# Carrying the last group's normalised heads into the rows of the others by transfers, in an attention and feed-forward kernel

## The chip, the cores and the metric
One core of a Trainium2 chip runs the whole program. The metric is the device time of one execution in microseconds (us). The engines are PE (TensorE, matrix products), DVE (VectorE), ACT (ScalarE), POOL (GpSimd) and SP (SyncE, which here only issues transfers). Each has a queue of its own that it works in order; they meet at semaphores.

## The reference
Input x is 2 x 2048 x 256 in float32. What is computed, cut down:

```
Q, K, V = x Wq^T, x Wk^T, x Wv^T          # 16 heads of 16 columns
O = causal softmax(Q K^T / 4) V, per head  # blocks of 128 keys in the reference
x = layernorm(x + O Wo^T)
lhs_scale = max|x| over a row / 127 ; rhs_scale = max|F| over a column / 127
acc = round(x / lhs_scale) @ round(F / rhs_scale)   # int8 values, clipped to 127
x = layernorm(x + acc * lhs_scale * rhs_scale)
```

## The kernel before
**Groups and steps.** The 2 x 16 heads are worked off as 8 groups of 4 heads (HG). A group covers one batch's 2048 tokens in 4 chunks of 512 queries (CH); chunk c meets key blocks kb = 0 to 4c + 3. This gives NS = 40 steps a group, 320 in all (ALL); FIRST = 0, 4, 12, 24 are the steps at which the chunks start in a group. In the last 4 steps of a chunk the width falls from 512 to 384, 256 and 128 (the diagonal). Step k issues on PE four score products, one for each head (L681, `product`), with three PSUM banks in turn; ACT takes the exponential of each (L1003) into PR. The products with the values (L734, `values_half`) follow two steps later (LAG) in two halves, behind scores 1 and 3. They add up in one bank, ps_acc, where head j has the rows from 32j: 16 rows of outputs and 16 of the sum of exponentials.

**Row maxima.** In groups 0 to 6 the queue of PE also holds, between the scores, the products for the row maxima of the next group (L681 into ps_max, `item`), which DVE reduces (L1072). The last group has none of them.

**The accumulator.** When a chunk's last values product is done, ACT copies ps_acc to accS[:, c % 2] (`copy_acc`, L993). This copy stands in ACT's queue behind the exponential of head 3 of the next chunk's step kb = 1. The first values product of the next chunk (step kb = 0, issued in step kb = 2) waits for it. In groups 0 to 6 SP then stores the four heads and the sums to DRAM (L456, L458).

**Ends of chunks.** When all 16 heads of a chunk of tokens are there, the chunk m (0 to 7, four of each batch) goes through projection with Wo, residual, layernorm, quantising, product with the int8 weights, residual, layernorm and store. This is done by halves of 256 tokens, e = 2m + s. Every operation of a half has a due step, written out in tables: HALF_START[e] plus an entry of DUE[e]. Each engine calls its part for the step that it is in (`end_parts` on DVE, ACT, POOL and SP; `between_scores` on PE in the last group). Within one step an engine does later stages of earlier halves first. Chunks 0 to 2 are worked within groups 4 to 6, chunk 3 at the start of the last group (halves 6 and 7 start at its steps 0 and 2).

**The joined chunks 4 to 7 (JOINED).** Their last four heads come from the last group itself. The 12 other heads are loaded from DRAM to o_in (128 rows in half h = 0, 64 rows in h = 1) and normalised by POOL with inverses spread in DRAM (`outputs`, L1383). The last four stay in accS: PE sums them to tokens by four small products with the tile `spread` (`token_sums`, L887), DVE inverts (`invert_last`, L1218, L1220), PE spreads the inverses over accS's rows by products with ident (`spread_inverses`, L899), DVE multiplies (`normalise_last`, L1226). The projection (`project`, `tiled`, L824) of one tile of 128 tokens is then three sets of four 32-column products: o_in half 0, o_in half 1 with 64 rows, and accS with wo_last, a copy of Wo's last 64 rows at the rows of accS (made by four transfers at the start). A half has two tiles. Of the joined chunks, 4, 5 and 6 have their copies at steps 5, 13 and 25 of the last group (COPIED), and their halves start at 7 and 9, 15 and 17, 27 and 29; token sums come at step 6, 14 and 26, spreads at the start of each half. Chunk 7 comes after the last score: its projection of o_in is done beforehand (L870) and finished with wo_last behind the others (`finish_projection`, L909).

**Order within a step of the last group.** Behind score j: `project` of tile j // 2 and half h = j % 2; with j = 0 the token sums and spreads (`joins`) and the turning of integers (`late_turn`, L845); with j = 2 the int8 product (`late_product`, L824 with ffn_q); with j = 1 and 3 the values.

Of the kernel before, what the change touches and what calls it, by code (L numbers as in the profile page):

```python
# [61 lines left out]
def build(nc, x, wq, wk, wv, wo, ffn, out):  # L62
# [45 lines left out]
    LAST_GROUP = (GROUPS - 1) * NS  # L108
    SOON_START = [NS * (GROUPS // B - 1 + m) + 26 for m in range(SOON)]
    JOINED = range(CHUNKS, ENDS)  # L110
    COPIED = [LAST_GROUP + FIRST[c] + 1 for c in range(1, CHUNKS)] + [ALL - 1]
    HALF_START = [at for at in SOON_START for s in range(2)] + [LAST_GROUP, LAST_GROUP + 2] + \
        [at for k in COPIED[:-1] for at in (k + 2, k + 4)] + [ALL + 1, ALL + 2]
    soon_chunk = lambda at: dict(sums_in=at - 17, sums_back=at - 14, load=at - 7, outputs=at - 2)
    CHUNK_DUE = [soon_chunk(at) for at in SOON_START] + [
        {part: LAST_GROUP + k for part, k in zip(("sums_in", "sums_back", "load", "outputs"), at)}
# [2 lines left out]
    def steps_of(**at):  # L119
# [10 lines left out]
                     product=28, residual2=29, rstd2=34, store=37)]  # L130
    LATE_DUE = dict(steps_of(mean=2, norm=4, mean2=11, norm2=13, gap=0), project0=0, project1=1, rstd1=3, to_int=6, turn=7,
                    take=7, product=8, scale=9, residual2=10, rstd2=12, store=14)
    JOIN_DUE = dict(LATE_DUE, spread=0, normalise=0, project0=1, project1=1)
    LAST_DUE = dict(LATE_DUE, spread=0, normalise=0, project0=-2, project1=-2, finish=1)
    DUE = [SOON_DUE[e % 2] if e < SOON_HALVES else LATE_DUE if e // 2 not in JOINED else JOIN_DUE if e < 2 * ENDS - 2
           else LAST_DUE for e in range(2 * ENDS)]
    DONE_AT = max(HALF_START[e] + max(DUE[e].values()) for e in range(2 * ENDS))

# [7 lines left out]

    def joins_due(k):

        return [m for m in JOINED if HALF_START[2 * m] - 1 == k]

    soon_due = lambda k, part: [e for e in due(k, part) if e < SOON_HALVES]
    late_due = lambda k, part: [e for e in due(k, part) if e >= SOON_HALVES]
# [109 lines left out]
    with ExitStack() as ctx:  # L262
# [89 lines left out]
        e_wo = sem("wo_last_in")  # L352
        e_wo_set = sem("last_constants")
        e_token = sem("sums_by_token")
        e_spread = sem("inverses_spread")
        e_last = sem("last_outputs_normalised")
        groups_under = lambda m: -(-(SLOT[m] - 1) * 3 * W // (TILES * GR))
# [35 lines left out]
        QSTEPS = 3 + TPH + 1  # L393
        late = lambda e: e - SOON_HALVES
        LAST_STEPS = 4
        joined = lambda m: m - JOINED[0]
        banks_of = lambda m: ps_score if m == ENDS - 1 else ps_max
        token_bank = lambda m: banks_of(m)[:, 0, 0:TPC * HG]
        spread_bank = lambda m, s: banks_of(m)[:, s, 0:HALF]
# [33 lines left out]
        with nc.Block() as block:  # L433
            @block.sync
            def _(sp):
# [43 lines left out]
                def end_parts(k):  # L479
                    for m in chunks_due(k, "sums_in"):  # L480
                        sums_in(m)
                    for m in chunks_due(k, "sums_back"):
                        sums_back(m)
                    for m in chunks_due(k, "load"):
                        load(m)
                    for e in due(k, "store"):
                        store_result(e)

# [39 lines left out]
                def load(m):  # L528
                    b, t0 = place(m)
                    if SLOT[m] >= 2:  # L530
                        sp.wait_ge(s_vg, CHUNKS * groups_under(m))
                    at_least(sp, e_out[SLOT[m]], 2 * 16 * (nth(m) - 1))
                    sp.wait_ge(e_back[SLOT[m]], 16 * nth(m))
                    for h in range(HALVES):
                        r, n = b * HEADS + h * (HEADS // HALVES), half_rows(m, h)
                        sp.dma_start(inv_in(m)[0:n, h, :], row_inv[m % CHUNKS, r:r + n // DH, :].unsqueeze(1)
                                     .broadcast_to([n // DH, DH, CH])).then_inc(e_in[SLOT[m]], 16)
                        sp.dma_start(o_in(m)[0:n, h, :], heads_out[r * DH:r * DH + n, t0:t0 + CH])\
                            .then_inc(e_in[SLOT[m]], 16)
                    sp.dma_start(work(m), x[b, t0:t0 + CH, :].rearrange("(t p) d -> p t d", p=P))\  # L540
                        .then_inc(e_x[SLOT[m]], 16)

                def sums_of(rows, m):

# [31 lines left out]
            def _(pe):  # L576
# [198 lines left out]
                def between_scores(k, j):  # L775


                    at = NS * (GROUPS - 1) + k
                    project(at, j // 2, j % 2)
                    if j == 0:  # L780
                        joins(at)
                        late_turn(at)
                    if j == 2:
                        late_product(at)
                    if j % 2:
                        values_half(*divmod(at - LAG, NS), j // 2)

                def soon_parts(k):

# [64 lines left out]
                def project(k, t, h):  # L854


                    for e in late_due(k, f"project{t}"):
                        m, s = divmod(e, 2)
                        if t == 0 and h == 0:
                            pe.wait_ge(e_on, HALVES * (m + 1))  # L860
                            pe.wait_ge(s_reduced, NI * GROUPS)
                            pe.wait_ge(e_res, e - 1)
                            if e == 2 * JOINED[0]:
                                pe.wait_ge(e_wo, 16 * HG)
                            if m in JOINED and m < ENDS - 1:
                                pe.wait_ge(e_last, LAST_STEPS * joined(m) + 3 + s)
                        at, n = s * HALF + t * P, half_rows(m, h)
                        rows = ps_max[:, s, t * D:t * D + D]
                        if m == ENDS - 1:
                            pe.matmul(rows, o_in(m)[0:n, h, at:at + P], wT[0:n, 3, h, :], start=t == 0 and h == 0, stop=False)  # L870
                            continue
                        last = h == HALVES - 1
                        y = tiled(rows, o_in(m)[0:n, h, at:at + P], wT[0:n, 3, h, :], h == 0, last and m not in JOINED)
                        if last and m in JOINED:
                            y = tiled(rows, accS[:, m % 2, at:at + P], wo_last[:, :], False, True)
                        if last:
                            y.then_inc(e_y, 1)

                def token_sums(m):
# [24 lines left out]
                def finish_projection(e):  # L904
                    m, s = divmod(e, 2)
                    pe.wait_ge(e_last, LAST_STEPS * joined(m) + 3 + s)
                    for t in range(TPH):
                        at = s * HALF + t * P
                        pe.matmul(ps_max[:, s, t * D:t * D + D], accS[:, m % 2, at:at + P],  # L909
                                  wo_last[:, :], start=False, stop=t == TPH - 1).then_inc(e_y, 1)  # L910
# [22 lines left out]
            def _(act):  # L933
# [53 lines left out]
                def copy_acc(g, c):  # L987
                    act.wait_ge(s_pv, NS * g + LAST[c] + 1)
                    if g < GROUPS - 1 or c < 2:
                        at_least(act, s_ost[c % 2], OST * (CHUNKS // 2 * g + c // 2))  # L990
                    else:
                        act.wait_ge(e_y, TPH * late(2 * (JOINED[c - 2] + 1)))
                    act.copy(accS[:, c % 2, :], ps_acc[:, :]).then_inc(s_accS, 1)  # L993

                def group(g):
                    for k, (c, kb) in enumerate(STEPS):
                        w = CH - skip(c, kb)
                        for j in range(HG):
                            use = score_use(g, k, j)
                            act.wait_ge(s_st, use + 1)  # L1000
                            if j == 0:
                                at_least(act, s_pv, NS * g + k - 3)
                            act.activation(PR[:, k % 4, j, 0:w], ps_score[:, bank_of(use), 0:w], ACT.Exp,  # L1003
                                           scale=SCALE).then_inc(s_exp, 1)
                            if kb == 1 and j == HG - 1 and (g or c):
                                copy_acc(g if c else g - 1, (c - 1) % CHUNKS)
                        soon_parts(NS * g + k)
                        end_parts(NS * g + k)
# [422 lines left out]
```

## Time and profile before
| | us |
|---|---|
| median of 3 runs (lowest, highest) | 1008.3 (1007.88, 1009.81) |
| the profiled execution | 1007.38 |
| its span in the trace | 1005.7 |
| busy: PE, DVE, ACT, POOL | 944.5, 799.5, 719.9, 272.0 |
| front part, up to the first steady group | about 120 |
| steady groups | 98 to 105 each |
| from step 4 of the last group to its last score | 863.74 to 976.11 |

The profile shows one execution. The profiled execution's own time is 1.7 us above its span; what lies between is start and end around the recorded work. A "quad" is four products of 32 columns each that run side by side in PE; a quad in float32 is recorded as 8 matmuls (two records for each), one in bf16 as 4. "x8" in a row of PE counts such records. The time of a row ends with its last record, which overlaps the next row; what a quad occupies is the distance between starts.

### The profile page before, as it was taken

What the parts mean: (1) busy time and instruction counts of PE and PEld (TensorE: products, weight loads), DVE (VectorE), ACT (ScalarE), POOL (GpSimd) and SP (SyncE); (2) the same over time, 40 slices, a digit from 0 to 9 for tenths busy, and PEclk for the clock granted to TensorE, in tenths of its full rate; (3) what the DMA queues carried; (4) which work ended last, traced back from release to release, by engine and by line L of the source; (5) the groups of instructions that cost most, each with busy time, mean ns of one, the idle gap of its engine ahead of it and who ended that gap; (6) DMA issues with size and microseconds to landing.
All of it is one profiled execution on the core that took longest, in us unless ns stands there. A gap on an engine that the chain in (4) does not pass through costs nothing.

```text
span 1005.7 us, 41095 instructions
## 1 busy us (share of the span) xinstructions
PE 944.5 (94%) x18208; PEld 590.9 (59%) x18208; DVE 799.5 (80%) x1081; ACT 719.9 (72%) x1494; POOL 272.0 (27%) x443
## 2 busy tenths in 40 slices
PE   8989999999999999999999999999999999879993
PEld 5645556656765676566656675666666654444441
DVE  5488888887888788878889898999899899365426
ACT  3423458788788878887878877887787887757670
POOL 4433452102210221021213230333124212353322
PEclk9999999999999999999999999999999999989995
DMA  5565440002210220022302230124013114502101
GB/s 177 161 200 159 157 125 15 5 9 53 69 32 9 60 68 24 9 58 80 83 6 60 64 116 8 40 76 114 19 34 78 50 33 112 114 14 75 34 2 42
DMA packets 70865, 66.47 MB, mean 66 GB/s; under 512 B 14704, under 2 KB 65200, under 8 KB 70688
## 3 DMA queue, kind: packets, MB, share of 16 engines
q1 hardware_dynamic: 70688, 63.84, 22.8%
q8 instruction: 143, 2.34, 1.0%
q14 instruction: 34, 0.28, 0.1%
HBM read 42.43 MB, written 20.91 MB: 63 GB/s over the span
## 4 chain that ended last, share of the span: by engine, by line
PE 77%; DVE 10%; ACT 6%; SPq 3%; issue 2%; POOL 1%; DMA 1%; POOLq 0%; ACTq 0%; DVEq 0%
PE ps_acc L734 20%; PE ps_score L681 19%; PE ps_max L681 18%; DVE block_max L1072 6%; PE ps_score L604 5%; ACT PR L1003 4%; PE ps_score L611 3%; PE ps_max L824 2%; PE ps_max L679 2%; SPq L439 2%; PE ps_max L699 2%; PE ps_score L824 1%; ACT accS L993 1%; PE ps_acc L585 1%; DVE end_slots L1183 1%
## 5 line engine op out<-in xcount | busy, mean ns | idle before, releaser
L1072 DVE TENSOR_REDUCE block_max<-ps_max 128x2 f32<-128x1024 f32 (+3 forms) x640 | 654.3, 1059 | 113.3 <-PE ps_max L681 56.7
L1003 ACT ACTIVATE PR<-ps_score 128x512 f32<-128x512 f32 (+3 forms) x1280 | 627.2, 539 | 160.4 <-PE ps_score L681 141.7
L681 PE MATMUL ps_score<-QS,KS 99*32 99x512 bf16 (+3 forms) x5120 | 452.3, 350 | 3.3 <-ACT PR L1003 2.2
L734 PE MATMUL ps_acc<-PR,VG 128*32 128x256 f32 (+1 forms) x5104 | 367.7, 350 | 10.5 <-ACT accS L993 9.1
L681 PE MATMUL ps_max<-KS,QS 96*32 96x512 bf16 (+3 forms) x4544 | 335.1, 348 | 5.5 <-DVE block_max L1072 2.9
L681 PEld LDWEIGHTS ps_score<-QS,KS 99*32 99x32 bf16 x5120 | 169.4, 96 | 96.5 <-ACT PR L1003 22.5
L734 PEld LDWEIGHTS ps_acc<-PR,VG 128*32 128x32 f32 x5104 | 170.2, 110 | 83.7 <-ACT PR L1003 16.2
L681 PEld LDWEIGHTS ps_max<-KS,QS 96*32 96x32 bf16 x4544 | 138.5, 96 | 88.4 <-DVE block_max L1072 37.7
L1318 POOL TENSOR_SCALAR_AFFINE_SELECT PR<-PR 128x512 f32<-128x512 f32 x128 | 82.8, 647 | 284.3 <-ACT PR L1003 284.1
L699 PE MATMUL ps_max<-mask_q,ident_b 128*32 128x96 bf16 (+3 forms) x1808 | 99.1, 200 | 0.0
L699 PEld LDWEIGHTS ps_max<-mask_q,ident_b 128*32 128x32 bf16 x1808 | 60.7, 97 | 10.0
L1326 POOL CAST max_parts<-neg_max 16x128 bf16<-16x128 f32 (+1 forms) x30 | 8.9, 297 | 195.1 <-ACT neg_max L985 193.1
L604 PE MATMUL ps_score<-PR,wT 128*128 128x512 f32 x128 | 60.3, 597 | 0.8 <-ACT neg_max L963 0.8
L945 ACT CAST end_slots<-ps_score 128x512 bf16<-128x512 f32 x32 | 18.7, 585 | 56.7 <-PE ps_score L604 56.7
L1305 POOL TENSOR_TENSOR end_slots<-PR,end_slots 128x512 bf16<-128x512 f32 x32 | 37.0, 1155 | 78.3 <-ACT end_slots L950 78.3
L679 PE MATMUL ps_max<-KS,QS 96*128 96x512 bf16 (+3 forms) x144 | 35.9, 345 | 7.1 <-DVE block_max L1072 7.0
L604 PEld LDWEIGHTS ps_score<-PR,wT 128*128 128x128 f32 x128 | 23.3, 190 | 20.6 <-issue 18.0
L1355 POOL TENSOR_SCALAR var_eps<-moments 128x2 f32<-128x2 f32 x32 | 7.4, 231 | 86.3 <-DVE moments L1178 86.3
L611 PE MATMUL ps_score<-wT,PR 128*128 128x256 f32 x128 | 30.0, 381 | 0.0
L1172 DVE BATCH_NORM_STATS2 stats<-end_slots 128x6 f32<-128x256 f32 x48 | 19.0, 417 | 12.0 <-POOL end_slots L1374 11.8
L1121 DVE TENSOR_TENSOR PR<-ps_score,end_slots 128x512 f32<-128x512 f32 x32 | 21.7, 683 | 8.0 <-ACT end_slots L945 6.9
L679 PEld LDWEIGHTS ps_max<-KS,QS 96*128 96x128 bf16 x144 | 13.3, 97 | 24.3 <-DVE block_max L1072 13.1
(125 smaller groups left out, 558.5 us busy)
## 6 DMA issues: line engine op xcount, KB each, us to landing
QS<-qparts SPq DMA_DIRECT2D x192, 64.0 KB, 2.4
KS<-kparts SPq DMA_DIRECT2D x192, 64.0 KB, 2.3
qparts<-end_slots SPq DMA_DIRECT2D x16, 384.0 KB, 3.8
kparts<-end_slots SPq DMA_DIRECT2D x16, 384.0 KB, 3.1
PR<-in_L_attn_x SPq DMA_DIRECT2D x8, 512.0 KB, 4.3
heads_out<-accS SPq DMA_DIRECT2D x112, 32.0 KB
end_slots<-in_L_attn_x SPq DMA_DIRECT2D x6, 512.0 KB, 7.5
out_y<-end_slots SPq DMA_DIRECT2D x12, 256.0 KB, 2.1
```

Source lines behind the costliest of these rows:

```text
L604: m = pe.matmul(bank, wT[:, w, mh, nh * P:nh * P + P], xT[:, n % 2, mh, :], start=mh == 0, stop=mh == HALVES - 1)
L611: m = pe.matmul(bank[:, t * D:t * D + D], xT[:, n % 2, mh, tile * P:tile * P + P], wT[:, 2, mh, :], start=mh == 0, stop=mh == HALVES - 1)
L679: return pe.matmul(bank[:, 0:w], stack, moving, start=True, stop=stop)
L681: m = pe.matmul(bank[t * QW:t * QW + QW, 0:w], stack[:, t * QW:t * QW + QW], moving, start=True, stop=stop)
L699: m = pe.matmul(bank[r:r + QW, w - P + r:w], ident_b[:, r:r + QW], mask_q[:, r:P], start=False, stop=True)
L734: m = pe.matmul(ps_acc[EYE * j:EYE * j + EYE, a:b], VG[:, kb, j, :], PR[:, k % 4, j, a - s:b - s], start=kb == 0 and a == 0, stop=k == LAS ...
L824: y = pe.matmul(out[r:r + QW], stack[:, r:r + QW], moving, start=start, stop=stop)
L1003: act.activation(PR[:, k % 4, j, 0:w], ps_score[:, bank_of(use), 0:w], ACT.Exp, scale=SCALE).then_inc(s_exp, 1)
L1072: dve.tensor_reduce(block_max[:, h * PAIR:h * PAIR + PAIR, i, b], ps_max[:, slot_at:slot_at + PAIR, 0:w], AX.X, ALU.max).then_inc(s_reduce ...
L1121: dve.tensor_tensor(rest[:, q % RESTS, :], ps_score[:, u % 3, :], parts[:, n % 2, u, 0, :], ALU.subtract)\
L1305: pool.tensor_tensor(parts[:, n % 2, u, 2, :], rest[:, q % RESTS, :], parts[:, n % 2, u, 1, :], ALU.subtract).then_inc(part3, 1)
L1318: pool.affine_select(out=block, in_=block, compare_op=ALU.is_ge, fill=0.0, base=0, pattern=[[0, HG], [1, P]], channel_multiplier=-1).then_ ...
```

## The change
Four edits:
1. For chunks 4 to 6, when both halves of accS have been multiplied, SP copies the four heads' rows by four transfers (`join_heads`) into the rows 64 to 127 of o_in half 1, which were unused. The projection of these chunks is then two sets of products with 128 rows; the products with wo_last are left to chunk 7 alone. PE waits for the transfers (e_join) before a half's first projection, and ACT's copy to a buffer that was joined waits for them too.
2. These halves start three steps later (10 and 12, 18 and 20, 30 and 32), their two tiles are projected in two steps, and both halves are spread in one step (7, 15, 27) and multiplied in the next (8, 16, 28), where the transfers are due too. Everything else of these halves moves three steps later with them: the last of chunk 6 comes to steps beyond the last score.
3. Token sums and spreads stand behind the values at the end of a step (j = 3), the turning of integers behind score 3.
4. In all groups, the copy of the accumulator stands behind the exponential of head 2 of its step, not of head 3.

```diff
-        [at for k in COPIED[:-1] for at in (k + 2, k + 4)] + [ALL + 1, ALL + 2]
+        [at for k in COPIED[:-1] for at in (k + 5, k + 7)] + [ALL + 1, ALL + 2]
...
-    JOIN_DUE = dict(LATE_DUE, spread=0, normalise=0, project0=1, project1=1)
+    JOIN_DUE = [dict(LATE_DUE, spread=-3, normalise=-2), dict(LATE_DUE, spread=-5, normalise=-4, join=-4)]
...
-        return [m for m in JOINED if HALF_START[2 * m] - 1 == k]
+        return [m for m in JOINED if COPIED[joined(m)] + 1 == k]
...
+                    for e in due(k, "join"):
+                        join_heads(e // 2)
                     for e in due(k, "store"):
                         store_result(e)
...
+                def join_heads(m):
+
+                    sp.wait_ge(e_last, LAST_STEPS * (joined(m) + 1))
+                    for j in range(HG):
+                        r = P - GR + j * DH
+                        sp.dma_start(o_in(m)[r:r + DH, HALVES - 1, :], accS[EYE * j:EYE * j + DH, m % 2, :])\
+                            .then_inc(e_join, 16)
...
-                    if j == 0:
-                        joins(at)
-                        late_turn(at)
                     if j == 2:
                         late_product(at)
+                    if j == 3:
+                        late_turn(at)
                     if j % 2:
                         values_half(*divmod(at - LAG, NS), j // 2)
+                    if j == 3:
+                        joins(at)
...
-                            if e == 2 * JOINED[0]:
-                                pe.wait_ge(e_wo, 16 * HG)
                             if m in JOINED and m < ENDS - 1:
-                                pe.wait_ge(e_last, LAST_STEPS * joined(m) + 3 + s)
-                        at, n = s * HALF + t * P, half_rows(m, h)
+                                pe.wait_ge(e_join, 16 * HG * (joined(m) + 1))
+                        at, n = s * HALF + t * P, half_rows(m, h) if m == ENDS - 1 else P
...
-                        last = h == HALVES - 1
-                        y = tiled(rows, o_in(m)[0:n, h, at:at + P], wT[0:n, 3, h, :], h == 0, last and m not in JOINED)
-                        if last and m in JOINED:
-                            y = tiled(rows, accS[:, m % 2, at:at + P], wo_last[:, :], False, True)
-                        if last:
+                        y = tiled(rows, o_in(m)[0:n, h, at:at + P], wT[0:n, 3, h, :], h == 0, h == HALVES - 1)
+                        if h == HALVES - 1:
                             y.then_inc(e_y, 1)
...
-                        act.wait_ge(e_y, TPH * late(2 * (JOINED[c - 2] + 1)))
+                        act.wait_ge(e_join, 16 * HG * (c - 1))
...
-                            if kb == 1 and j == HG - 1 and (g or c):
+                            if kb == 1 and j == HG - 2 and (g or c):
                                 copy_acc(g if c else g - 1, (c - 1) % CHUNKS)
```

## Rows read from the trace of the kernel before

**Rows 1.** The page: busy time, share of the span and instructions.
```profile
PE 944.5 (94%) x18208; PEld 590.9 (59%) x18208; DVE 799.5 (80%) x1081; ACT 719.9 (72%) x1494; POOL 272.0 (27%) x443
```

**Rows 2.** Busy time by stretch: start:end, length, engines, PE clock, DMA share, GB/s.
```profile
550.00:655.00 105.00, 102.65 (x2320) 67.66 (x2312) 94.03 (x126) 85.32 (x184) 30.24 (x54) 1.00 0.22 60
863.74:976.11 112.37, 99.16 (x1729) 50.38 (x1717) 57.58 (x169) 79.01 (x163) 39.03 (x57) 0.94 0.21 52
```

**Rows 3.** Waits of PE and weight loads, 120 to 868: total, times, longest.
```profile
PE ps_acc L734 <- ACT accS L993: 9.1, 21, 0.6
...
PEld ps_max L681 <- DVE block_max L1072: 37.7, 113, 1.1
```

**Rows 4.** Timeline, a copy within a group: start, length, what [idle before].
```profile
250.35 0.22 PE L734 MATMUL ps_acc<-PR,VG 128*32 128x64 f32 x1
...
251.01 0.58 ACT L993 COPY accS<-ps_acc 128x512 f32<-128x512 f32 x1
...
251.73 0.64 PE L734 MATMUL ps_acc<-PR,VG 128*32 128x256 f32 x8 [0.49 <-ACT accS L993]
```

**Rows 5.** Timeline, the last values product before a copy at a group's start.
```profile
242.47 0.29 PE L734 MATMUL ps_acc<-PR,VG 128*32 128x64 f32 x8
```

**Rows 6.** Waits of PE, 862 to 985, the last group.
```profile
PE ps_max L899 <- DVE last_sums L1220: 4.0, 1, 4.0
PE ps_max L887 <- ACT accS L993: 3.5, 3, 1.2
PE ps_max L845 <- ACT end_slots L1051: 2.3, 3, 0.9
PE ps_max L845 <- ACT V L1051: 1.1, 2, 0.8
...
PE ps_max L824 <- DVE accS L1226: 0.7, 1, 0.7
```

**Rows 7.** Timeline of PE and weight loads, one tile's projection.
```profile
878.84 0.61 PE L824 MATMUL ps_max<-wT,V 128*32 128x256 f32 x8
879.27 0.62 PE L824 MATMUL ps_max<-ffn_q,end_slots 128*32 128x256 bf16 x16
...
880.03 0.15 PEld L824 LDWEIGHTS ps_max<-wT,V 64*32 64x32 f32 x8 [0.32 <-issue]
...
880.60 0.64 PE L824 MATMUL ps_max<-wo_last,accS 128*32 128x256 f32 x8
```

**Rows 8.** Timeline of ACT, three plain steps.
```profile
955.06 5.99 ACT L1003 ACTIVATE PR<-ps_score 128x512 f32<-128x512 f32 x12 [1.19 <-PE ps_score L681]
```

**Rows 9.** Busy time by stretch, as rows 2, one of three where the clock is low.
```profile
903.23:906.70 3.47, 3.47 (x52) 2.23 (x56) 1.07 (x3) 1.19 (x2) 0.00 (x0) 0.50 0.11 35
```

**Rows 10.** Normalising, issue (ns min/median/max), landing (KB each, median us).
```profile
875.82 0.41 DVE L1226 TENSOR_TENSOR accS<-accS,ps_max 128x256 f32<-128x256 f32 x1
...
L456 SPq DMA_DIRECT2D heads_out<-accS x112: 303/421/1669, 152.9 to 861.9; - x112
...
wo_last<-wT SPq DMA_DIRECT2D x4, 16.0 KB, 2.4
...
end_slots<-in_L_attn_x SPq DMA_DIRECT2D x2, 512.0 KB, 8.3
```

**Rows 11.** The chain of waits from the last values to half 14.
```profile
977.29 2.51 PE ps_max L870 x8
...
985.33 0.70 DVE end_slots L1272
```

**Rows 12.** The same chain, later.
```profile
996.49 1.07 PE ps_max L824 x14
997.58 0.89 DVE end_slots L1248 x2
998.54 1.27 POOL end_slots L1374
999.84 0.76 DVE stats L1172 x2
```

More of the change, by code:

```diff
@@ L110, in build @@
     JOINED = range(CHUNKS, ENDS)
+    joined = lambda m: m - JOINED[0]
     COPIED = [LAST_GROUP + FIRST[c] + 1 for c in range(1, CHUNKS)] + [ALL - 1]
     HALF_START = [at for at in SOON_START for s in range(2)] + [LAST_GROUP, LAST_GROUP + 2] + \
-        [at for k in COPIED[:-1] for at in (k + 2, k + 4)] + [ALL + 1, ALL + 2]
+        [at for k in COPIED[:-1] for at in (k + 5, k + 7)] + [ALL + 1, ALL + 2]
     soon_chunk = lambda at: dict(sums_in=at - 17, sums_back=at - 14, load=at - 7, outputs=at - 2)
@@ L132, in build @@
                     take=7, product=8, scale=9, residual2=10, rstd2=12, store=14)
-    JOIN_DUE = dict(LATE_DUE, spread=0, normalise=0, project0=1, project1=1)
     LAST_DUE = dict(LATE_DUE, spread=0, normalise=0, project0=-2, project1=-2, finish=1)
-    DUE = [SOON_DUE[e % 2] if e < SOON_HALVES else LATE_DUE if e // 2 not in JOINED else JOIN_DUE if e < 2 * ENDS - 2
+    JOIN_DUE = [dict(LATE_DUE, spread=-3, normalise=-2), dict(LATE_DUE, spread=-5, normalise=-4, join=-4)]
+    DUE = [SOON_DUE[e % 2] if e < SOON_HALVES else LATE_DUE if e // 2 not in JOINED else JOIN_DUE[e % 2] if e < 2 * ENDS - 2
            else LAST_DUE for e in range(2 * ENDS)]
@@ L354, in build @@
         e_token = sem("sums_by_token")
+        e_join = sem("last_heads_joined")
         e_spread = sem("inverses_spread")
@@ L395, in build @@
         LAST_STEPS = 4
-        joined = lambda m: m - JOINED[0]
         banks_of = lambda m: ps_score if m == ENDS - 1 else ps_max
@@ L906, in finish_projection @@
                     pe.wait_ge(e_last, LAST_STEPS * joined(m) + 3 + s)
+                    if s == 0:
+                        pe.wait_ge(e_wo, 16 * HG)
                     for t in range(TPH):
```

## The prediction
> **What bounds the kernel now.** I began with the page: TensorE (PE) is busy for 94% of the span, ACT for 72%, and nothing else comes near [rows 1]. So the question is where PE has time that it loses. The table by stage splits it: in a steady stretch PE is busy for 102.65 of 105 us, in the stretch of the last group from step 4 to the last score, 863.74 to 976.11, for 99.16 of 112.37 us, at a mean clock of 0.94 [rows 2]. A steady group is one long PE queue. What PE itself waits for there is nearly one thing, the copy of the accumulator: 9.1 us in 21 waits [rows 3]. After the last score comes a chain of some 29 us across DVE, POOL, ACT and PE, in which every step counts [rows 11, 12]. The three stretches are costed apart. All terms are for the profiled execution: 1007.4 us with a span of 1005.7; the median of the runs is 1008.3, 0.9 more, and I add the change to that median.
>
> **The copy one head sooner (groups 0 to 6, and the joins between them).** The copy stands in ACT's order behind the exponential of head 3. At 251 us the last product of values of the old chunk ends near 250.6, yet the copy begins at 251.01, when the exponential of head 3 is through, and PE takes up the next product of values at 251.73, having waited 0.49 [rows 4]. One exponential takes 0.49 of ACT's queue (12 in 5.99, less the overlap of the last [rows 8]), so with the copy ahead of it PE finds the buffer free when it comes: the 0.49 goes. The exponential of head 3 ends when the copy ended before, and PE asks for its bank behind the next values product, past 252.1, so nothing replaces the wait. Not so where the chunk copied is the fourth of a group: the values product started at 242.47 and ran for 0.29, so the copy can't start before 242.8 wherever it stands, and it did start then [rows 5]; there PE's wait stays, and the exponential behind it comes 0.4 later, which PE's next scores just bear. Three of the 21 waits are of that kind (at the longest, 0.6, 1.7 us). 18 waits with 7.4 us can go. Some of it PE will hand on, since weight loads for the row maxima stand 37.7 us behind DVE [rows 3] and in the later groups DVE is busy for 94.03 of 105 us [rows 2]. Ends: 2 (DVE absorbs most) and 8; I take 5.5, near the upper one, since DVE has slack even there. **-5.5.**
>
> **The last group: waits of PE that go.** PE waits 3.5 us in three token sums for the copy, 4.0 in one spread for DVE's inverse, 0.7 for DVE's normalising, 2.3 and 1.1 in turns for ACT's integers [rows 6]. Token sums move from the start to the end of the step after the copy, about 1.7 us of PE work later, and the copy is a head sooner: all 3.5 go. The spread of 4.0 waited because DVE was inside the norm-to-round block of the half before, which started its step earlier; now the projections start three steps later, so at that join DVE has only second norms left: 4.0 goes. The 0.7 goes with its wait. Turns stand behind score 3 now, whose bank is free only after the integers were made; but 1.9 of their 3.4 us lie between 960 and 968, where ACT sets the pace (below), so I take 1.0 of them. **-9.2.**
>
> **The products with wo_last.** One tile's projection was three groups in PE: heads 0 to 7 (878.84 to 879.27, 0.43), the 64 rows of the other half (880.03 to 880.60, 0.57, with about 0.1 lost ahead of it), and accS with wo_last (0.46); the weights of the 64-row group are not loaded ahead, its load row shows a gap of 0.32 [rows 7]. Together 1.57 us. With 128 full rows it is twice 0.43, 0.87: 0.70 less for a tile, and there are 12 such tiles (96 matmuls of wo_last, 8 for each): 8.4 us of PE work. What it is worth hangs on the step. A plain step is 8 quads of scores and values, 1.74 us of PE, while ACT's four exponentials take 1.96 to 2.0 (12 in 5.99 and PE paced by them) [rows 8]: there ACT is the bound. Before, both tiles of a half fell into one step: 1.74 + 3.13 = 4.87 of PE, and the step behind it was ACT's, 1.96: 6.83. Now the tiles fall into two steps of 1.74 + 0.87 = 2.61: 5.22. Six halves: 6 x 1.6 = **-9.7.** The normalise work of POOL and DVE is unchanged in amount. Bounds: 5 (if the weight gaps stay and ACT hides part) and 10.
>
> **The clock.** After the idle time at the token sums and the spread, PE ran at the half level (granted 0.50, that is 1.2 GHz) from 903.23 to 906.70 [rows 9]; there are three such stretches of 3.0 to 3.5 us in the last group, about 9.9 us in all, and half of it, 4.9 us, is lost. The idle time that goes is what came before these falls. Two thirds of it, **-3.2**: a new wait (next part) can make it fall once. The Trainium skill, "TensorE: Matmul & The Clock Gate", What's actually happening, has the same two levels and an idle stretch as the cause; by that rule a join that stops PE for long would bring the loss back, which is part of rival B.
>
> **The joins.** Each of three chunks adds four transfers of 32 KB on SP's queue and a wait of PE at the first projection. The chain: spreads at the end of a step; two normalises of 0.41; four issues at 0.42 each (1.7, as for the same rows into heads_out); a landing, for which the nearest row is the load of wo_last, also from SBUF to SBUF, 2.4 us; the lower end is a transfer that PE never waits for, the upper a landing of 8.3 (tokens, 512 KB) [rows 10]. I take 2.4, since the queues are quiet there (a DMA share of 0.21 [rows 2]). Sum 0.8 + 1.7 + 2.4 + 0.3 for handing over = 5.2 us. PE gets to the first projection after two steps and a score. A step takes the larger of ACT's 1.96 (0.5 more where it makes integers or takes a turn) and PE's 1.74 (0.43 more for an int8 product): 2.5 and 2.0 for steps 8 and 9 of the last group (chunk 4), 2.5 and 2.4 for 16 and 17, 2.2 and 2.0 for 28 and 29: 4.2 to 4.9, plus 0.2. For chunk 4 DVE is late besides: it norms to 875.8 as before [rows 10]. So the three waits are about 1.6, 0.4 and 1.0: **+3.0**, bounds 0 and 3 x 6 = 18. Behind the waiting projection PE holds scores, so ACT runs dry with it. Behind the join on SP stand the stores of finished halves and chunk 7's load, with steps to spare; ahead of chunk 5's stands the store of half 6 (step 14), whose norm is due at 13. [...]
> The copies of chunks 6 and 7 now wait for the joins of 4 and 5, due eight steps and more earlier: nothing.
>
> **Sum of the last group:** -9.2 - 9.7 - 3.2 + 3.0 = -19.1. 112.4 becomes 93.3, still above ACT's 79.0 busy [rows 2].
>
> **The tail.** Chunk 6 starts three steps later, so the product of its second half and DVE's work on both halves move behind the last score. (1) The product stands in PE's queue between the projection of 977.29, which ends at 979.80, and the token sums [rows 11]: 0.62 at full clock [rows 7], 1.07 at half [rows 12]; I take 0.6, since its overlap with the neighbours is worth some of the slower clock. (2) DVE's queue ahead of the residual of half 14 (985.33 [rows 11]) held one norm, one pair of stats and two normalises, and it still waited for L909. Now PE's token sums end at about 981.4, inverse and first spread at 982.7, then: normalise 0.4, stats and aggregate of half 12 0.76 + 0.25, two scalings 0.85 [rows 12], which ends at 984.9; POOL's residual of half 13 follows, behind its rstd, 0.2 + 1.27 to 986.35 [rows 12]; then stats and aggregate 0.95: the residual starts at 987.3 instead of 985.33, +2.0, with (1) in it. (3) Norm 2 of half 13 now stands ahead of norm 1 of half 14: +0.65. Together **+2.7**; ends 0.6 (only the product) and 5 (all 4.3 of moved DVE work and the product).
>
> **Total:** -5.5 - 19.1 + 2.7 = -21.9; 1008.3 - 21.9 = 986.4.
>
> **Rivals.** (A) The copy gains nothing in the steady groups: DVE, busy for up to 90% there, takes over the waits, or the held exponential costs what the copy gives. For it: 37.7 us of weight loads behind DVE [rows 3]; against: 11 us of 105 in which DVE is idle [rows 2]. The rest as forecast: -16.4, 992. (B) The wait at the joins takes the place of those removed: landings of 4 to 5 us, each wait 3 to 4, the clock falls as before and the 3.2 is not had: -21.9 + 8 + 3.2 = -10.7, 998. For it: the chain has no reserve at any of the three; against: wo_last's 2.4 [rows 10]. (C) The better end: the clock stays up all through, joins cost nothing, 7.4 is had: -21.9 - 1.9 - 1.7 - 3.0 = -28.5, 980. (D) Slower: the join on SP. It is one queue in order; if a join is held behind the store ahead of it or lands as the tokens do, at 8.3 us, PE stops 6.9 us at each and runs at half clock for 3.5 us behind each (1.75 lost): 3 x 8.65 = 26 instead of 3, no clock gain: -21.9 + 23 + 3.2 = +4.3, 1012.6. It decides from a landing of about 7 us. Against it: no transfer of this size behind so little traffic takes as long. That the change doesn't do what it says is hard to see: 96 matmuls leave PE whatever happens.
>
> **How the numbers follow.** Forecast (984 to 989.5) 0.38, A 0.17, B 0.21, C 0.17, D 0.03, and 0.04 for mishaps beyond these, shared by the three outcomes. The range from 979 to 999 holds C, A and most of B. A measurement of this kernel tells 0.2% (2 us) from no change: faster 0.94, same 0.02, slower 0.04.
>
> **What would show it.** No waits of L734 on accS but those at a group's start; no matmul with wo_last but in the tail; h=1 projections with 128 rows and no gap of the weight load; PE waits at L824 for the join of about 1 us; the clock at 1.00 from 890 on; 93 us from step 4 of the last group to its last score; the tail from the last value product to the end 2 to 3 us longer. Wrong if DVE waits of PE grow in the steady groups, if the join waits are above 3 us, or if the clock falls at other places.

## The result and the profile after

The changed kernel takes 991.8 us (median of 4 runs, 990.22 to 994.13) where the kernel before took 1008.45: a ratio of 0.9835, 95% interval 0.9812 to 0.9858, or 16.6 us less. The forecast was 21.9 us less: 986.4, in a range of 979 to 999. The profiled execution took 992.43 us with a span of 990.7, 15.0 less than the span before.

The page (shares as in [rows 1]), then the busy time by stretch (columns as in [rows 2]); the second stretch runs, as there, from step 4 of the last group to the last values:

```profile
PE 935.6 (94%) x18112; PEld 589.1 (59%) x18112; DVE 799.9 (81%) x1081; ACT 716.3 (72%) x1494; POOL 271.9 (27%) x443
```
```profile
550.00:655.00 105.00, 103.76 (x2361) 68.67 (x2352) 95.26 (x126) 86.08 (x185) 31.38 (x56) 1.00 0.22 62
861.42:958.25 96.83, 88.66 (x1616) 49.97 (x1604) 55.24 (x163) 76.93 (x162) 38.24 (x56) 0.96 0.25 64
```

PE has 96 records fewer, those of wo_last. In the steady stretch PE is busy for 103.76 of 105 us (102.65 before), in the last group for 88.66 of 96.83 (99.16 of 112.37): the stretch shrank by 15.5 us and PE's work by 10.5.

The best ruler is ACT's copy of the accumulator, which both kernels make 32 times: the same copy marks the same place of the work in both. These are the copies of chunks 4 to 7 in the last group of the changed kernel, from ACT's timeline (start, length, idle before; the first row is the last copy of group 6):

```profile
856.89 0.58 ACT L1002 COPY accS<-ps_acc 128x512 f32<-128x512 f32 x1 [0.47 <-PE ps_acc L745]
866.43 0.63 ACT L1002 COPY accS<-ps_acc 128x512 f32<-128x512 f32 x1
887.87 0.58 ACT L1002 COPY accS<-ps_acc 128x512 f32<-128x512 f32 x1 [0.26 <-PE ps_acc L745]
921.99 0.58 ACT L1002 COPY accS<-ps_acc 128x512 f32<-128x512 f32 x1 [0.61 <-PE ps_acc L745]
959.50 0.58 ACT L1002 COPY accS<-ps_acc 128x512 f32<-128x512 f32 x1 [0.56 <-PE ps_acc L745]
```

| us | before | after | difference | forecast |
|---|---|---|---|---|
| first copy to the last of group 6 | 707.38 (152.26 to 859.64) | 704.97 (151.92 to 856.89) | -2.4 | -5.5 |
| first to last copy of the last group | 108.46 (868.90 to 977.36) | 93.07 | -15.4 | -19.1 |
| last copy to the end of the span | 28.3 | 31.2 | +2.9 | +2.7 |

**The steady groups.** PE's waits from 120 to 865 us, as in [rows 3]:

```profile
PE ps_max L692 <- DVE block_max L1081: 5.0, 9, 2.7
PE ps_score L692 <- ACT PR L1012: 3.0, 8, 0.6
PE ps_acc L745 <- ACT accS L1002: 1.8, 4, 0.5
```

Of 21 waits for the copy 4 are left, and their sum fell from 9.1 to 1.8 us. The copy of [rows 4] looks like this now, and there is no wait at the values product behind it (timeline: the last product of the old chunk, the copy, the first of the new one):

```profile
249.51 0.22 PE L745 MATMUL ps_acc<-PR,VG 128*32 128x64 f32 x1
...
249.81 0.58 ACT L1002 COPY accS<-ps_acc 128x512 f32<-128x512 f32 x1
...
250.54 0.64 PE L745 MATMUL ps_acc<-PR,VG 128*32 128x256 f32 x8
```

The lead over the kernel before is how much sooner the same copy starts. Within a group it grows by 0.3 to 0.5 us from copy to copy, at a group's start it shrinks by 0.25. At the copy of 445.66 it is 2.62, at 466.14 (469.87 before) 3.73. At the next, 499.82 (500.48), it is 0.66. Between them lies one long wait, the 2.7 of the first row above:

```profile
464.05 0.43 SPq L563 DMA_DIRECT2D sums<-row_sums  x1
...
467.33 0.20 DVE L1166 TENSOR_SCALAR sums<-sums 128x64 f32<-128x64 f32 x1 [2.29 <-DMA sums<-row_sums]
...
468.98 0.61 PE L692 MATMUL ps_max<-KS,QS 96*32 96x512 bf16 x8 [2.71 <-DVE block_max L1081]
```

DVE stood 2.29 us at the sums of chunk 0 for a transfer that SP issued at 464.05 and that was there at 467.3; PE then stood 2.71 us for DVE's maxima. Behind that wait the granted clock of PE fell (first row below, columns as in [rows 2]: 0.62 on average over the stretch; the other two rows are of the last group):

```profile
469.00:473.50 4.50, 4.50 (x55) 1.93 (x58) 2.03 (x3) 2.28 (x4) 0.00 (x0) 0.62 0.34 82
896.42:900.80 4.38, 4.38 (x52) 2.36 (x44) 4.08 (x13) 3.84 (x8) 1.01 (x2) 0.61 0.12 26
921.40:924.40 3.00, 3.00 (x46) 1.39 (x48) 2.83 (x11) 2.41 (x6) 1.72 (x3) 0.57 0.26 87
```

**The last group.** PE's waits from 862 us on, as in [rows 6] (the lines that matter for chunks 4 to 7; 9.0 us of the first is in the tail):

```profile
PE ps_max L857 <- ACT end_slots L1060: 9.5, 2, 9.0
PE ps_score L692 <- ACT PR L1012: 2.1, 3, 1.4
PE ps_max L906 <- DVE V L1281: 1.9, 1, 1.9
PE ps_acc L745 <- POOL PR L1327: 1.8, 2, 1.3
PE ps_max L836 <- ACT end_slots L1050: 1.4, 2, 0.7
PE ps_max L836 <- POOL V L1392: 1.0, 1, 1.0
...
PE ps_max L836 <- DMA end_slots<-accS: 0.4, 1, 0.4
```

The token sums' 3.5, the normalising's 0.7 and the turns' waits in the group are gone. In place of the spread's 4.0 stand 1.9 for a residual (L1281), and new is a score that waits 1.4 for ACT, at 920.46. Where that comes from, DVE and ACT say (timeline):

```profile
919.29 0.63 ACT L1060 ACTIVATE V<-V 128x512 bf16<-128x512 f32 x1 [1.26 <-DVE V L1221]
...
920.46 0.55 PE L692 MATMUL ps_score<-QS,KS 99*32 99x512 bf16 x4 [1.39 <-ACT PR L1012]
```

ACT stands 1.26 us for DVE's rounding of half 10, with its exponentials queued behind; PE has filled its three banks and stands too. Part of DVE's lateness is a meeting with POOL. The small product for lscale takes DVE 0.17 us at 893.32 and 899.19; here it takes 1.08 and ends when POOL's residual of another half ends (timeline):

```profile
916.53 1.27 POOL L1383 TENSOR_TENSOR V<-V 128x512 f32<-128x512 f32 x1
...
916.75 1.08 DVE L1206 TENSOR_SCALAR lscale<-amax 128x2 f32<-128x2 f32 x1
```
That is 0.9 of the 1.26 us. The joins cost about 1.4: 1.0 at chunk 4 (the table gives it to POOL's L1392, which ended at about the same time; that instruction is chunk 5's, and most later executions put the same wait down to the transfer) and 0.4 at chunk 6.

A tile's projection is now two sets with 128 rows (881.82 and 882.31, each with another product behind it). There is no gap, and a set occupies 0.43 to 0.44 us:

```profile
881.82 0.64 PE L836 MATMUL ps_max<-wT,V 128*32 128x256 f32 x8
882.25 0.27 PE L692 MATMUL ps_score<-QS,KS 99*32 99x128 bf16 x4
882.31 0.64 PE L836 MATMUL ps_max<-wT,V 128*32 128x256 f32 x8
882.75 0.53 PE L745 MATMUL ps_acc<-PR,VG 128*32 128x192 f32 x8
```

**The tail.** The chain of waits from the last copy on, as [rows 11]:

```profile
961.95 0.55 PE ps_max L836 x16
962.50 1.00 PE ps_score L894 x8
...
967.24 1.67 DVE end_slots L1192 x2
968.91 0.67 DVE stats L1181 x2
...
969.85 0.59 DVE end_slots L1281
```

The int8 product stands ahead of the token sums (0.55), then DVE's norm and statistics of halves 12 and 13 ahead of the residual of half 14. That residual starts 10.3 us behind the last copy; before it was 8.0 (977.36 to 985.33). The norm of 967.24 is another meeting with POOL, whose residual runs from 967.18 to 968.44: 1.67 us, where two such operations take 0.73 elsewhere in the tail.

### The profile page after: what moved, and what is told of

Its sections match the earlier page's. It is cut to its first block, busy times and chain, and to the rows that moved or that the text cites. A ratio compares the mean times of both kernels' runs of the same rounds, so it can differ in the third digit from the quotient of the medians.

```text
span 990.7 us, 40916 instructions
## 1 busy us (share of the span) xinstructions
PE 935.6 (94%) x18112; PEld 589.1 (59%) x18112; DVE 799.9 (81%) x1081; ACT 716.3 (72%) x1494; POOL 271.9 (27%) x443
## 4 chain that ended last, share of the span: by engine, by line
PE 77%; DVE 10%; SPq 6%; ACT 3%; issue 2%; POOL 1%; DMA 1%; POOLq 0%; DVEq 0%; ACTq 0%
PE ps_acc L745 20%; PE ps_score L692 20%; PE ps_max L692 18%; DVE block_max L1081 6%; PE ps_score L615 5%; SPq L440 4%; PE ps_score L622 3%; PE ps_max L690 2%; ACT PR L1012 2%; PE ps_max L836 2%; PE ps_max L710 1%; PE ps_score L836 1%; SPq L457 1%; PE ps_acc L596 1%; DVE end_slots L1192 1%
## 5 line engine op out<-in xcount | busy, mean ns | idle before, releaser
L1192 DVE TENSOR_SCALAR end_slots<-end_slots,moments,rstd 128x256 f32<-128x256 f32 x48 | 20.9, 459 | 9.4 <-POOL rstd L1367 9.4
```

The costliest lines, as they stand in the source:

```text
L1192: dve.tensor_scalar(dst[:, at, :], src[:, at, :], moments[:, z, which, at, 0:1], rstd[:, z, which, at:at + 1], ALU.subtract, ALU.mult).the ...
```

## The experiments

Eleven kernels in three rounds. Those of a round shared their runs of the kernel before, whose medians were 1008.07 us (experiments 1 to 4), 1006.88 (5 to 8) and 1008.06 (9 to 11). A difference of about 1 us between medians of different rounds is therefore not safe; each ratio is to the kernel before in its own round.

**1. The copy alone.** On the kernel before:
```diff
-                            if kb == 1 and j == HG - 1 and (g or c):
+                            if kb == 1 and j == HG - 2 and (g or c):
```


> The kernel before with one edit of the four alone: the accumulator is copied behind the exponential of head 2. Theory (the copy's gain builds up at 0.3 to 0.5 us a copy until about 470 us, 3.7 us by then in the changed kernel, and is then given back where DVE waits for the sums' transfer): by the end of group 6 about 2.5 us earlier than before, and in the last group the three token sums still wait, but 0.5 us less each; in all 3 to 5 us, 1004. Rival (DVE takes over the waits everywhere, and the steps of the last group gain nothing from the copy): 1 us at most, 1007.5. As the prediction had it (5.5 in the steady groups): 1002.

Measured: 1001.21 us, ratio 0.9928 (0.9901 to 0.9955). First copy to the last of group 6: 702.19, 5.2 us less; last group 107.5, 1.0 less; tail the same. The prediction's 5.5 fits. The idea of the expectation, that the gain is given back at the sums as a consequence of the copy, fell here: this kernel has the copy and waited only 0.37 us for the sums.

**2. All but the copy.** The changed kernel with the reverse of that edit.

> The changed kernel with the copy put back behind the exponential of head 3. Theory: the steady groups lose their 2.3 us and the 3.1 us given back at 470 to 500 don't arise, because DVE then comes to the sums after they have landed; the first values product of chunks 1 to 3 in the last group waits 0.5 longer each. In all 2.5 to 4 us slower than the changed kernel, 995. Rival (the copy is worth nothing, the last group all): 992, the same as the changed kernel.

Measured: 997.61, ratio 0.9889 (0.9858 to 0.9919): 5.8 slower than the changed kernel. And DVE waited 2.5 us for the sums, without the sooner copy: the steady groups took 4.3 us more than in the kernel before. So the wait hangs on when the transfer lands. In the thirteen profiled executions of this document it was there 1.9 to 2.1 us after its issue in ten, and 3.3 to 3.5 in three (the changed kernel, experiment 2, and the kernel of experiment 9). The program around it is the same in the changed kernel and in experiment 4, where it came early:

```profile
463.95 0.42 SPq L563 DMA_DIRECT2D sums<-row_sums  x1
465.90 0.20 DVE L1171 TENSOR_SCALAR sums<-sums 128x64 f32<-128x64 f32 x1 [0.43 <-DMA sums<-row_sums]
```
The two rows are experiment 4's. What makes the landing late in some executions stays open.

**3. The inverses later,** on the changed kernel:
```diff
-    soon_chunk = lambda at: dict(sums_in=at - 17, sums_back=at - 14, load=at - 7, outputs=at - 2)
+    soon_chunk = lambda at: dict(sums_in=at - 17, sums_back=at - 12, load=at - 7, outputs=at - 2)
```


> The changed kernel with the inverses of the first batch's sums two steps later on DVE (sums_back at - 12 instead of at - 14), so that DVE comes to them after the transfer has landed. Theory (a wait of DVE for the sums of 2.3 us, taken over by PE as 2.7 us and paid again in 3 us at the half clock, gave back 3.1 us of the copy's gain): no wait of DVE for the sums, no half clock at 470 to 474, the end 3 us sooner, 989, and the start of step 4 of the last group 5.4 us earlier than in the kernel before instead of 2.3. Rival (DVE is the bound of groups 4 to 6 and takes over whatever comes free): the wait goes, and the end stays at 991 to 992.

Measured: 989.72, ratio 0.9812 (0.9785 to 0.9839). DVE inverts at 468.35 without a wait; the first copy is at 152.02, the last of group 6 at 852.78: 700.76, 6.6 less than before. This execution alone doesn't show that the two steps of reserve help, since its transfer landed after 1.9 us. The kernel of experiment 9 shows it: it has the later inverses too, and its transfer landed 3.3 us after the issue, at 468.5, still ahead of DVE:

```profile
465.19 0.43 SPq L569 DMA_DIRECT2D sums<-row_sums  x1
...
468.99 0.18 DVE L1172 TENSOR_SCALAR sums<-sums 128x64 f32<-128x64 f32 x1
```
It lost nothing there: 701.08 us from the first copy to the last of group 6. The median of experiment 3 is 2.1 better, less than the 3 expected. That would fit a wait that not every execution has, but the intervals of the two ratios overlap, so the size of the gain is not settled.

**4. wo_last kept.** The changed kernel without `join_heads`, with the projection's third set of products as before:
```diff
-                                pe.wait_ge(e_join, 16 * HG * (joined(m) + 1))
+                                pe.wait_ge(e_last, LAST_STEPS * joined(m) + 3 + s)
...
+                        if last and m in JOINED:
+                            y = tiled(rows, accS[:, m % 2, at:at + P], wo_last[:, :], False, True)
```


> The changed kernel with the products of wo_last kept in the projections of chunks 4 to 6 and no transfers to o_in; steps, order and copy as changed. Theory of the prediction (the 12 times 0.70 us of PE work are worth their full amount, since all twelve lie in steps that PE bounds, less the waits for the transfers of 1.4 us that go): 6 to 7 us slower than the changed kernel, 998.5. Rival (the steps and waits made the gain, ACT covers the work): within 2 us of the changed kernel, 993.

Measured: 992.77, ratio 0.9846 (0.9819 to 0.9873), 1 us above the changed kernel, within the spread of the runs: the rival's number, not the theory's. Its copies in the last group:

```profile
862.92 0.63 ACT L1007 COPY accS<-ps_acc 128x512 f32<-128x512 f32 x1
885.95 0.58 ACT L1007 COPY accS<-ps_acc 128x512 f32<-128x512 f32 x1 [0.95 <-PE ps_acc L745]
920.09 0.58 ACT L1007 COPY accS<-ps_acc 128x512 f32<-128x512 f32 x1
959.59 0.58 ACT L1007 COPY accS<-ps_acc 128x512 f32<-128x512 f32 x1 [0.56 <-PE ps_acc L745]
```
From the first to the last it is 96.67 us, 3.6 more than with transfers (93.07). The profiled executions take nearly the same in all (992.55 and 992.43), since this one did not have the late landing and was 3.5 us shorter in the steady groups. From chunk 5's copy to chunk 6's it is 34.14 against 34.12: the saved products of the four tiles between them, 2.8 us of PE work, brought no time. The stretch tells why (busy by stretch, wo_last kept):

```profile
885.95:920.09 34.14, 30.66 (x572) 15.62 (x564) 18.85 (x56) 25.84 (x54) 10.52 (x16) 1.00 0.20 48
893.40:897.50 4.10, 3.62 (x72) 1.84 (x72) 3.93 (x14) 3.16 (x7) 1.01 (x2) 1.00 0.22 68
```
The clock stays at 1.00, also behind the spread that waits 1.7 us here; with the transfers it is 0.93 over the stretch. No score waits longer than 0.4 us for ACT here, against 1.4 with the transfers. So PE did its extra products at full clock in the time in which it otherwise stood and ran at half.

**5 to 8. Repairs,** on top of the later inverses (989.7 in the round before; the kernel before was 1.2 us lower in this round). Residual sooner:
```diff
-    ... dict(LATE_DUE, spread=-5, normalise=-4, join=-4)]
+    ... dict(LATE_DUE, spread=-5, normalise=-4, join=-4, residual=1, stats1_0=1, stats1_1=1, aggr1=1)]
```


> The kernel with the later inverses (989.7) and, besides, the residual and statistics of the second half of each joined chunk one step sooner on DVE, ahead of the first half's norm-to-round block instead of behind it. Theory (at chunk 5 the second spread waits 1.9 us for the bank that this residual has to read, and the clock falls behind it in some executions): that wait goes, from the copy of chunk 5 to that of chunk 6 the stretch shrinks from 33.5 by 2 to 3 us, 987.5. Rival (ACT or the integers set the pace of this stretch, the wait is handed on to the integers of half 10): the stretch stays within 0.7 us, 989.5.

Measured: 989.35, ratio 0.982 (0.9801 to 0.9838): no gain. The spread's wait is gone, but (timeline) PE stands at the join of chunk 5 instead, and ACT waits longer still for the integers of half 10, since the residual of half 11 now stands ahead of half 10's norm on DVE, and that norm meets POOL's residual (1.99 us at 910.66):

```profile
914.93 0.63 ACT L1061 ACTIVATE V<-V 128x512 bf16<-128x512 f32 x1 [2.77 <-DVE V L1222]
```
```profile
895.95 0.64 PE L837 MATMUL ps_max<-wT,V 128*32 128x256 f32 x8 [1.12 <-DMA V<-accS]
...
916.10 0.62 PE L693 MATMUL ps_score<-QS,KS 99*32 99x512 bf16 x4 [2.90 <-ACT PR L1013]
```

Integers of chunk 5 later:
```diff
+    later = lambda due: {part: at + (part in LATER) for part, at in due.items()}   # LATER: to_int and what follows
+    DUE = [later(JOIN_DUE[e % 2]) if e // 2 == 5 else SOON_DUE[e % 2] ...
```


> The kernel with the later inverses (989.7) and, besides, everything of chunk 5 from the integers on one step later. Theory (the integers of half 10 are due two narrow steps behind the norm, 2.2 us after it, while DVE needs 4.3: ACT waits 1.3 us for them, its exponentials run dry and PE with them, 1.4 us, and the clock may fall): ACT's wait for the integers goes, the exponential that kept PE from its score for 1.4 us too; stretch 33.5 shrinks by 1 to 1.5, and the later clock falls behind the copy of chunk 6 go, 1 to 1.5: 987.5. Rival (the mask on POOL and the copy stand there as well, so PE waits for them instead): 989.5.

Measured: 987.25, ratio 0.9797 (0.9777 to 0.9816). By the medians that is 2.5 us better, by the ratios 1.5. In the trace the last group, first to last copy, takes 90.82 us instead of 93.12; of this the stretch from chunk 5's copy to chunk 6's gives 1.9 (31.64 instead of 33.54).

The tail in other steps:
```diff
+    for e, at in ((12, dict(scale=8, residual2=9, stats2_0=9, stats2_1=9, aggr2=9, rstd2=10, norm2_0=11, norm2_1=11, store=14)),
+                  (13, dict(scale=7, residual2=8, stats2_0=10, stats2_1=10, aggr2=10, rstd2=11, norm2_0=15, norm2_1=15, store=16))):
+        DUE[e] = dict(DUE[e], **at)
```


> The kernel with the later inverses (989.7) and, besides, the last parts of chunk 6 in other steps: the scaling of half 13 and the statistics of half 12 ahead of DVE's wait for the last token sums, norm 2 of half 13 behind the rounding of half 15. Theory of the prediction (the tail grew by 2.9 us since DVE's work on chunk 6 stands between the last inverse and the residual and norm of half 14): from the last copy to the end 28 to 28.5 instead of 31.2 us, 986.9. Rival (the product of half 13 on PE and the clock there make the tail longer): 30.5 us, 989.

Measured: 986.73, ratio 0.9794 (0.9774 to 0.9813). By the medians that is 3.0 us better, by the ratios 1.8. From the last copy (957.30) to the end it takes 27.8 us instead of 31.2, less than in the kernel before, though the product of half 13 still stands ahead of the token sums. DVE scales half 13 in the time in which it waits for these, and the norm that met POOL takes 0.73 again (timeline):

```profile
960.34 0.88 DVE L1260 SCALAR_TENSOR_TENSOR end_slots<-ps_max,lscale,ffn_scale 128x256 f32<-128x256 f32 x2 [1.84 <-PE ps_max L839]
961.31 0.17 DVE L1230 TENSOR_SCALAR last_sums<-ps_score 128x16 f32<-128x16 f32 x1
```

All four:

> All of them: later inverses, residual sooner, integers of chunk 5 later, the tail in other steps. If each is worth what its theory says, they add: 989.7 - 2.2 - 2.2 - 2.8 = 982.5. If the rivals hold for the first two, 987.

Measured: 983.22, ratio 0.9758 (0.9725 to 0.9791), with runs from 980.42 to 986.06: by the medians the sum of what each was worth alone (989.7 - 0.4 - 2.5 - 3.0 = 983.8).

**9 to 11. What is left.** The later inverses, the later integers and the tail's steps, without the earlier residual; the same with wo_last kept (the edit of experiment 4); the same with the earlier residual for half 9 alone.

> Later inverses, integers of chunk 5 later and the tail in other steps, but not the earlier residual. Theory (the earlier residual of half 11 holds up DVE's norm of half 10, as it did when it was made alone, and the waits that it takes away come back at the join and the integers): no slower than all four together (983.2), 982.5. Rival (with the integers later the earlier residual is worth its 1.9 us): 985.

Measured: 983.46, ratio 0.9752 (0.9737 to 0.9766), the same as all four.

> As the kernel with three repairs and no earlier residual, but with wo_last's products kept and no transfers. Theory (the transfers save 8.4 us of PE work, of which 3.3 were lost to falls of the clock and 1.4 to waits for the transfers; with the integers later one fall and its wait are gone, so the work counts more): from the first to the last copy of the last group 5 us longer than with transfers, 987. Rival (that stretch is set by ACT and DVE, the PE work was never worth more than 3.6): 3.5 us longer or less, 985.5.

Measured: 989.83, ratio 0.9817 (0.9801 to 0.9833). The pair, with and without transfers (ACT's timeline, the first copy and the last of the group):

```profile
862.81 0.63 ACT L1008 COPY accS<-ps_acc 128x512 f32<-128x512 f32 x1
...
953.61 0.58 ACT L1008 COPY accS<-ps_acc 128x512 f32<-128x512 f32 x1 [0.56 <-PE ps_acc L751]
```
```profile
862.77 0.63 ACT L1013 COPY accS<-ps_acc 128x512 f32<-128x512 f32 x1
...
959.74 0.58 ACT L1013 COPY accS<-ps_acc 128x512 f32<-128x512 f32 x1 [0.56 <-PE ps_acc L751]
```
90.80 and 96.97: the transfers are worth 6.2 us here, against 3.6 in experiment 4 (the theory said 5, the rival at most 3.5). The clock is at 1.00 in both stretches, so the 8.4 us of products come through but for the join waits (1.4) and 0.8.

> As the kernel with three repairs, and the earlier residual for half 9 alone, which is the one that the second spread of chunk 5 waits for; half 11 is left. Theory (the spread's wait of 1.9 us goes, a join wait of 1 us comes in its place, and the integers are not held up): 1 us faster than without it, 981.5. Rival (handed on in full): 982.5, the same.

Measured: 983.67, ratio 0.9751 (0.9734 to 0.9768): by the medians the rival, the wait is handed on. The runs leave it unclear, though. The profiled execution was the fastest of the four (981.58, the others 983.01 to 984.57), and its last group took 89.18 us against 90.80 in experiment 9, as the theory had it.

The best versions are those with three repairs, with or without an earlier residual, which the runs don't tell apart: 983.5 us, 24.6 below the kernel before in its round and about 8 below the changed kernel.

## Why the prediction was right, and where its size was off

**Direction and range** held; the gain was three quarters of the forecast. By its own steps:

- *The copy, -5.5.* Right: 5.2 alone, 5.9 (experiment 4, 701.51) and 6.6 (experiment 3) with the rest. Its two halves held as well: the waits within a group went, those at a group's start stayed (4 left, where the prediction counted 3), and the lead shrinks by 0.25 there. The profiled execution shows only 2.4, since it lost 3.1 to the late landing, a term that was not in the sum. [rows 3] holds waits of PE and of weight loads alone; DVE had a wait of 0.4 us for this transfer in the kernel before, that is, the place had no reserve.
- *Waits that go, -9.2.* Less the 1.9 of the residual 7.3 are left. The step that failed is "at that join DVE has only second norms left". The inverse did come at once, but the second spread goes into the bank that half 9's residual has yet to read, and on DVE this residual stands behind half 8's norm-to-round block: 1.9 us. Experiment 5 took it away and got nothing, since the join of chunk 5 and half 10's integers were next, as late by as much.
- *wo_last, -9.7, and the joins, +3.0.* The work was right (10.5 us less busy in the stretch, in which half-clock time counts double). The joins cost 1.4 instead of 3.0: the landing took 2.0 us instead of 2.4, but the four issues took 2.4 to 2.7 instead of 1.7, so the chain was as long as forecast. What differed is when PE came, and for chunks 5 and 6 the prediction's own step times give waits of 0.1 and 0.8 where it took 0.4 and 1.0.
- *What the transfers alone gave.* The terms say 8.4 - 3.0 = 5.4, the pair of experiment 4 says 3.6; the sum of the larger of ACT's and PE's time in each step took no account of DVE. This is the step that was missing from the sum. With the steps moved, the integers of half 10 fell two narrow steps (about half the time of full ones) behind their norm, and DVE's block from norm to round, 4.4 us (914.87 to 919.26), did not fit. ACT stood for it, then PE. That is the wait that took the place: 1.4 us, worth 1.5 to 2.5 when repaired. The block of half 8 took 3.1 us (891.73 to 894.81); of the 1.3 more, 0.9 is the meeting with POOL shown above. An estimate from these rows: without it ACT would have waited some 0.4 us. No experiment moved POOL's work, so the share of each is not tested. Nor was the splitting of a half's tiles over two steps, part of the 9.7, run alone.
- *The clock, -3.2.* It fell twice, not once: (1 - 0.61) x 4.38 + (1 - 0.57) x 3.00 = 3.0 us lost of the former 4.9, so -1.9. Each fall came behind one of the two waits just named, and the longer one behind 1.9 us of standing. The reading of the kernel before was partly wrong: its three stretches are two falls. The first came at about 896.6 us, behind token sums that had waited 1.15 us (894.90), and before the wait of 4.0 us; the clock then stayed low through that wait, to 906.7. Columns as in [rows 2]:

```profile
899.30:903.20 3.90, 0.00 (x0) 0.00 (x0) 3.70 (x8) 0.60 (x1) 2.63 (x3) 0.50 0.00 0
```
- The three together: 1.9 + 1.4 + 1.3 - 1.6 (joins) = 3.0 of the 3.7 that the last group fell short. The other 0.7 is not traced, and the parts overlap, so this is an account and not a measurement of each.
- *The tail, +2.7.* Right, +2.9, and for the reason given: moving those instructions brought 3.4 us back (31.2 to 27.8). But 0.9 of the 2.9 is the norm that met POOL, which the sum did not have.
- *Rivals.* A fell (experiments 1 and 3). B named the right kind, a new wait and the clock, at the wrong place: the joins cost no more than either of the other two. C fell too: the joins cost something, and the clock did not stay up. D never came near: the landing was 2.0 us.
- *Signs of being wrong.* Two of the three named came. DVE's waits of PE in the steady groups grew from 2.9 to 5.0 us, by the one of 2.7 at the sums, and the clock fell at another place (469 us) and was not at 1.00 from 890 on. The stretch took 96.8 us, not 93. The total is within 5.3 us of the forecast because the errors were small, and because the joins' 1.6 lay on the other side from the rest.

## What to carry to other kernels

When steps of a schedule are moved against work of changing width, check every hand-over again in microseconds, not in steps: three steps later can mean two narrow ones in a row. A sum over steps of the larger of two engines misses the third that feeds both; write its time between "due" and "needed" beside it. And a transfer that lands just in time is a risk to be priced even when the trace shows 0.4 us for it: two steps of reserve cost nothing here, and with them a landing of 3.3 us passed without a wait. Last, look at what POOL does while DVE is on the critical chain: twice a DVE operation became 0.9 us longer beside POOL's work.

## What was not expected of the hardware

- The same transfer of the sums (row_sums to sums), issued at the same place of the program, landed after 1.9 to 2.1 us in ten profiled executions and after 3.3 to 3.5 in three. Where DVE had no reserve, that cost 3 to 4 us by the end of group 6, through DVE, PE and the clock.
- A wait of 1.7 us at the second spread left the clock at 1.00 (experiment 4), one of 1.9 us at the same place was followed by 4.4 us at 0.61 (the changed kernel), and with the same wait of 1.9 us in experiment 3 the clock stayed at 1.00 from there to 916 us. Of six profiled executions with a wait of 1.9 to 2.0 us there (the changed kernel, experiments 2, 3, 6, 7 and 9) two had the fall behind it, the changed kernel and experiment 2. So the length of PE's standing alone does not decide it, and a term for the clock needs a range of its own.
- DVE's small TENSOR_SCALAR for lscale (L1206, 128x2) takes 0.17 us, but 1.08 when it starts 0.2 us into POOL's TENSOR_TENSOR on 128x512, and it ends with that, at 917.8. In experiment 3 it is 1.07 us, in 6 and 9 1.08, each time in the same company. In experiment 4 another DVE operation meets POOL's, the rounding (L1226): 1.38 us instead of 0.43.
